# Q and k pieces taken from PSUM by TensorE and ScalarE, a third bank pair for the wide scores, and filler matmuls

## What is computed

```python
qkv = x @ w_attn                       # 16 query heads of 8, one k and one v head of 8
att = softmax(mask(q k^T * scale))     # causal, 256 x 256 per head
x = x + (att @ v) @ w_proj             # on layernorm(x)
sim = einsum(q', keys)                 # 8 heads, 2 x 32 key scores per token
sx, ix = top_k(sim[0], 16); sy, iy = top_k(sim[1], 16)
scores, pk = top_k(all pairs sx + sy, 16)
h = gelu(xn . table_down[indices]) * softmax(scores)
x = x + sum(h * table_up[indices])
```

## Time and profile before

| | us |
|---|---|
| median of 3 runs | 883.25 (880.9 to 883.42) |
| profiled execution | 882.14 |
| its span | 880.4 |
| TensorE busy | 725.1 (82%) |
| VectorE busy | 752.1 (85%) |
| ScalarE busy | 704.5 (80%) |
| GpSimd busy | 646.6 (73%) |
| mean granted TensorE clock | 0.953 of full speed |

### The profile page before, as it was taken

The page is one execution under the profiler, slowest core; times in us unless marked ns, Lnnn a source line. Parts: engine busy times, 40 slices in busy tenths (PEclk is TensorE's granted clock), DMA queues, the critical chain, the costliest instruction groups (busy, mean ns, idle before and its releaser), DMA issues.

```text
span 880.4 us, 20930 instructions
## 1 busy us (share of the span) xinstructions
PE 725.1 (82%) x6084; PEld 483.2 (55%) x6116; DVE 752.1 (85%) x2962; ACT 704.5 (80%) x959; POOL 646.6 (73%) x370
## 2 busy tenths in 40 slices
PE   3987688897979798897979798897979788876767
PEld 2653345564746465564646465564646465553646
DVE  4428799899989898999989898989989898988884
ACT  1365788989889898989989898989989898869471
POOL 3111596997969697997969697897969696887662
PEclk9897889999999999999999999999999999799988
DMA  6223021210302121210302121210302021000000
GB/s 180 45 39 73 1 59 21 53 31 18 66 0 65 18 58 25 52 31 12 71 0 65 18 58 25 52 31 11 72 0 65 18 53 26 25 8 6 15 6 7
DMA packets 34736, 32.53 MB, mean 37 GB/s; under 512 B 5520, under 2 KB 32784, under 8 KB 32976
## 3 DMA queue, kind: packets, MB, share of 16 engines
q1 hardware_dynamic: 34608, 32.12, 16.4%
q10 hardware_dynamic: 96, 0.02, 0.0%
HBM read 19.93 MB, written 5.24 MB: 29 GB/s over the span
## 4 chain that ended last, share of the span: by engine, by line
PE 29%; issue 29%; DVE 21%; ACT 10%; POOL 7%; ACTq 1%; another core or an unknown queue 1%; POOLq 1%; DVEq 1%; DMA 0%
DVE prob L1050 8%; PE score L1373 6%; ACT prob L744 4%; POOL acc L510 4%; DVE late_scores L905 3%; ACT late_scores L610 3%; PE misc L1444 3%; PE misc L1290 2%; PE score L1270 2%; PE score L1385 2%; DVE halves L899 2%; DVE ranked L949 1%; PE score L1327 1%; PE misc L1393 1%; PE score L1272 1%
## 5 line engine op out<-in xcount | busy, mean ns | idle before, releaser
L510 POOL TENSOR_TENSOR acc<-acc,prob 128x1024 f32<-128x1024 f32 x184 | 435.4, 2366 | 16.2 <-DVE prob L1050 0.5
L1050 DVE SCALAR_TENSOR_TENSOR prob<-score,cut,prob 128x1024 f32<-128x1024 f32 x256 | 317.9, 1279 | 31.9 <-ACT prob L744 30.6
L744 ACT ACTIVATE prob<-score,neg_lse,unit 128x1024 f32<-128x1024 f32 x256 | 301.4, 1203 | 27.6 <-PE score L1373 22.4
L1373 PE MATMUL score<-sel,pieces_t 128*128 128x512 f16 x512 | 161.6, 402 | 57.6 <-DVE prob L1050 54.9
L510 POOL TENSOR_TENSOR acc<-prob 128x1024 f32<-128x1024 f32 x32 | 75.6, 2362 | 100.7 <-DVE prob L1050 100.7
L637 ACT ACTIVATE probs<-score 128x512 f32<-128x512 f32 x192 | 109.8, 597 | 24.2 <-PE score L1272 20.2
L1373 PEld LDWEIGHTS score<-sel,pieces_t 128*128 128x128 f16 x512 | 40.5, 102 | 118.8 <-DVE prob L1050 107.6
L1327 PEld LDWEIGHTS score<-xn_kept,wdt 128*128 128x128 f32 x480 | 72.4, 191 | 29.7 <-issue 6.7
L1327 PE MATMUL score<-xn_kept,wdt 128*128 128x128 f32 x480 | 85.0, 278 | 3.9 <-DVE prob L1050 3.5
L1444 PEld LDWEIGHTS misc<-wu,gated_t 128*128 128x128 f32 x480 | 65.1, 199 | 13.8 <-DVE qk_rest L892 5.8
L1240 PE MATMUL score<-k_ahead,q_ahead 128*128 128x256 bf16 (+1 forms) x512 | 68.9, 246 | 2.9 <-ACT late_scores L610 0.7
(11 more groups left out here) (147 smaller groups left out, 1424.7 us busy)
## 6 DMA issues: line engine op xcount, KB each, us to landing
q_scratch<-qk_piece SPq DMA_DIRECT2D x16, 192.0 KB, 2.1
q_ahead<-q_scratch SPq DMA_DIRECT2D x16, 192.0 KB
q_stack<-q_scratch SPq DMA_DIRECT2D x16, 192.0 KB
xin<-x SPq DMA_DIRECT2D x16, 128.0 KB, 2.4
q_ahead<-q_scratch SPq DMA_DIRECT2D x16, 128.0 KB
q_stack<-q_scratch SPq DMA_DIRECT2D x16, 128.0 KB
xres<-x SPq DMA_DIRECT2D x16, 128.0 KB, 2.6
x_kept<-x SPq DMA_DIRECT2D x16, 128.0 KB, 2.0
```

What stands on the lines that cost most here:

```text
L510: eng.tensor_tensor(acc[:, j, :], so_far, prob[:, j * FH + h, :], ALU.add).then_inc(acc_added, FH - h if last else 1)
L744: eng.activation(prob[:, g, :], score[g % BUFS][:, :], ACT.Exp, bias=neg_lse[:, j, h:h + 1], scale=unit[:, :]).then_inc(prob_made, 1)
L1050: eng.scalar_tensor_tensor(prob[:, g, :], score[g % BUFS][:, :], cut[:, j, h:h + 1], prob[:, g, :], ALU.is_ge, ALU.mult).then_inc(prob_mas ...
L1373: ins = eng.matmul(score[g % BUFS][:, cols], pieces_t[:, j, h, :], sel[:, cols], start=True, stop=True)
```

## The change

1. **Pieces of q and k.** VectorE's and GpSimd's subtractions go. TensorE subtracts the piece just copied from the bank itself, with a negated identity (`take_piece`); ScalarE copies the middle and the low piece from the bank.
2. **Scale.** The scale of the exp is rounded to a power of two and put into the selection matrix (`sel_unit`, bfloat16); the exp keeps only its bias tile. The cut is scaled by VectorE (`scale_cut`).
3. **Bank pairs.** The six wide score groups use banks 2, 1, 2, 1, 2, 0. The first stands ahead of the value products, and tile 1's transposed sum ahead of the last group and of the piece transposes.
4. **Softmax steps** are done once for both tiles, with the copied maxima in `score[0]`.
5. **Filler matmuls** (`keep_busy`): 9, 4 and 3 where TensorE waits.
6. The order on ScalarE and VectorE follows these.

```diff
-                eng.activation(qk_piece[:, 1, :], qk_rest[:, :], ACT.Copy).then_inc(qk_middle, 1)
+                eng.activation(qk_piece[:, 1, :], misc[1][:, :], ACT.Copy).then_inc(qk_middle, 1)
+            def qk_low_piece(b):
+                eng.wait_ge(qk_last_made, every(qk_last_made, b))
+                eng.activation(qk_piece[:, 2, :], misc[1][:, :], ACT.Copy).then_inc(qk_low, 1)
...
-                eng.activation(prob[:, g, :], score[g % BUFS][:, :], ACT.Exp, bias=neg_lse[:, j, h:h + 1],
-                               scale=unit[:, :]).then_inc(prob_made, 1)
+                eng.activation(prob[:, g, :], score[g % BUFS][:, :], ACT.Exp,
+                               bias=neg_lse[:, j, h:h + 1]).then_inc(prob_made, 1)
...
+            def take_piece(b, n):
+                if n == 0:
+                    eng.wait_ge(setup_dve, 4)
+                    eng.wait_ge(qk_high, every(qk_high, b))
+                else:
+                    eng.wait_ge(qk_middle, every(qk_middle, b))
+                eng.matmul(misc[1][:, :], neg_ident_bf[:, :], qk_piece[:, n, :], start=False,
+                           stop=True, skip_group_check=True).then_inc(qk_last_made if n else qk_rest_made, 1)
```

ScalarE's order in an iteration:

```diff
+                if m:
+                    max_scores_back(i + 2, 0)
                 if a:
                     invert_sums(i + 1)
                 if m:
-                    copy_v(i + 2)
-                    max_scores_back(i + 2, 0)
                     max_scores_back(i + 2, 1)
-                if f:
-                    best_exp(i, 0)
-                if m:
                     max_scores_back(i + 2, 2)
                     max_scores_back(i + 2, 3)
                 if a:
                     x2_back(i + 1)
                 if f:
+                    best_exp(i)
+                if m:
+                    max_scores_back(i + 2, 4)
+                    max_scores_back(i + 2, 5)
+                if f:
+                    log_sum(i)
                     pieces_back(i, 0)
-                if m:
-                    max_scores_back(i + 2, 4)
-                if f:
-                    log_sum(i, 0)
-                if m:
-                    max_scores_back(i + 2, 5)
-                if f:
                     pieces_back(i, 1)
+                if f:
+                    pair_probs(i, 0, 0)
                 if a:
                     xn_back(i + 1)
-                if f:
-                    pair_probs(i, 0, 0)
-                    best_exp(i, 1)
                 if p:
                     xhat_back(i + 3)
                 if f:
                     pair_probs(i, 0, 1)
-                    log_sum(i, 1)
+                if m:
+                    copy_v(i + 2)
+                if f:
                     pair_probs(i, 0, 2)
...
                 if f:
                     pair_probs(i, 0, 7)
+                if p:
+                    qk_low_piece(i + 3)
                 if m:
                     max_back(i + 2)
```

VectorE's order:

```diff
                     select_pairs(i, 0)
-                    shift_best(i, 0)
                     sum_pairs(i, 1)
-                if d and f and not a:
+                    select_pairs(i, 1)
+                if a:
+                    make_y(i + 1)
+                if d and f:
                     gate(i - 1, 0)
                 if f:
-                    select_pairs(i, 1)
-                if a:
-                    make_y(i + 1)
-                if d and a:
-                    gate(i - 1, 0)
+                    shift_best(i)
                 if a:
                     norm_x2(i + 1)
                 if p:
                     ln1(i + 3)
-                if f and not a:
-                    shift_best(i, 1)
-                if f:
-                    sum_best(i, 0)
+                if f:
+                    bound_sizes(i)
+                    sum_best(i)
                 if d and f:
                     gate(i - 1, 1)
-                if f and a:
-                    shift_best(i, 1)
-                if f:
-                    log_sum_exp(i, 0)
-                if m:
-                    fold_max(i + 2, 0, 3)
-                if f:
-                    bound_sizes(i)
-                if m:
-                    fold_max(i + 2, 3, 4)
-                if f:
-                    sum_best(i, 1)
-                if m:
-                    fold_max(i + 2, 4, 5)
+                if m:
+                    fold_max(i + 2, 0, 1)
+                if f:
+                    log_sum_exp(i)
+                if m:
+                    fold_max(i + 2, 1, 2)
                 if f:
                     place_cut(i)
                 if m:
-                    fold_max(i + 2, 5, 6)
+                    fold_max(i + 2, 2, 4)
+                if f:
+                    scale_cut(i)
+                if m:
+                    fold_max(i + 2, 4, 6)
                 if f:
                     mask(i, 0, 0)
-                    log_sum_exp(i, 1)
                     mask(i, 0, 1)
                     mask(i, 0, 2)
                     mask(i, 0, 3)
                     mask(i, 0, 4)
                     mask(i, 0, 5)
-                if p:
-                    qk_remainder(i + 3)
```

TensorE's order:

```diff
+                if m:
+                    scores_for_max(i + 2, 0)
                 if a:
                     weigh_values(i + 1, 0, max_t_made, i + 1)
                     weigh_values(i + 1, 1, max_t_made, i + 1)
                 if m:
-                    scores_for_max(i + 2, 0, d)
-                    scores_for_max(i + 2, 1)
+                    scores_for_max(i + 2, 1, d)
+                    scores_for_max(i + 2, 2)
                 if d and f:
                     acc_transposes(i - 1, 0)
...
                     project_y(i + 1, y_t_made, i + 1)
+                if m:
+                    scores_for_max(i + 2, 4)
+                if d and f and a:
+                    acc_transposes(i - 1, 1, m)
+                if m:
+                    scores_for_max(i + 2, 5)
                 if f:
                     if a:
                         piece_transposes(i, 0, y_t_made, every(y_t_made, i + 1))
                     else:
                         piece_transposes(i, 0, sim_kept, every(sim_kept, i))
+                    if m:
+                        eng.wait_ge(x2_made, every(x2_made, i + 1))
+                        keep_busy(misc[1], 9)
                     piece_transposes(i, 1, piece_t_made, at(piece_t_made, i, 1))
-                if d and f and a:
-                    acc_transposes(i - 1, 1, m)
-                elif f and d:
+                if f and d and not a:
                     sum_late_tile()
...
                     for n in range(4, 7):
+                        if p and n == 6:
+                            take_piece(i + 3, 0)
                         pair_scores(i, 0, n, a, m)
...
                 if p:
+                    take_piece(i + 3, 1)
                     keep_busy(misc[0], 2)
...
                     if p:
-                        reader, of_batch = qk_rest_made, i + 3
+                        reader, of_batch = qk_low, i + 3
```

More of the change, by code:

```diff
@@ L7 @@
 FP16 = mybir.dt.float16
+INT32 = mybir.dt.int32
 ALU = mybir.AluOpType
@@ L42 @@
 WIDE_STEPS = 6
+MAX_BANK = (2, 1, 2, 1, 2, 0)
 BUFS = 3
@@ L203, in build @@
         qk_rest_made = signal("qk_rest_made")
+        qk_last_made = signal("qk_last_made")
         qk_middle = signal("qk_middle")
@@ L764, in prologue @@
                 xhat_back(2)
+                max_scores_back(1, 0)
                 invert_sums(0)
-                for w in range(2):
-                    max_scores_back(1, w)
+                max_scores_back(1, 1)
                 x2_back(0)
@@ L1197, in fold_keys @@
                 eng.wait_ge(weights_in, 6 * 16)
+                eng.wait_ge(max_kept, every(max_kept, 0))
                 for l in range(LISTS):
@@ L1228, in scores_for_max @@
                     eng.wait_ge(ahead_in, every(ahead_in, b))
+                    if later(b):
+                        eng.wait_ge(att_probs, at(att_probs, b, 0))
+                elif w == 1:
                     if d:
                         eng.wait_ge(act_made, every(act_made, b - 3))
-                elif w == 1:
-                    if later(b):
-                        eng.wait_ge(att_probs, at(att_probs, b, 0))
-                else:
+                elif w < 5:
                     eng.wait_ge(max_kept, at(max_kept, b, w - 1))
+                elif later(b - 1 if isinstance(b, int) else b):
+                    eng.wait_ge(shifted_made, every(shifted_made, b - 2))
                 for u in (2 * w, 2 * w + 1):
-                    bank = score[1 + w % 2][:, (u % 2) * BANK:(u % 2 + 1) * BANK]
+                    bank = score[MAX_BANK[w]][:, (u % 2) * BANK:(u % 2 + 1) * BANK]
                     nh, nk, h0, j = (4, P, 4 * u, 0) if u < 4 else (2, T, 2 * (u - 4), 1)
@@ L1357, in pair_scores @@
                     eng.wait_ge(piece_t_made, at(piece_t_made, b, j + 1))
+                    if not later(b):
```

(5 more changed lines are left out.)

163 lines of the change are left out of this document (84 added, 79 removed).

## The result

The changed kernel takes **901.88 us** (median, 899.79 to 902.68) against 883.34 for the kernel before on the same chip: ratio 1.0208, 95% interval 1.0183 to 1.0234. It is slower, as forecast, by 18.5 us where the forecast had about 11. The median lies inside the range (871 to 902) by 0.1, at its edge, and above the likeliest case's own range (887 to 899). The profiled execution spans 899.8 us, 19.4 more than before.

The account below looks back on a forecast made before the run. The prediction took a loop of waits across engines as the bound, GpSimd's and ScalarE's loops nearly equal. 11 x 0.95 = 10.5, -2.5 and +4.2 gave +12.2 on 882.14: 894 us, range 871 to 902, likeliest case 887 to 899.

Parts of the forecast that it names:

- The first score group ahead: On TensorE, value products now await all twelve exps: +0.2 us on the path to xhat, bounds 0 and +0.54.
- GpSimd beside the folds: GpSimd's rstd, centring and scaling take 3.63 us instead of 2.97 beside VectorE's earlier fold: +0.66, bounds 0 and +1.3.
- The exps: On ScalarE, one operand tile fewer makes each exp 0.09 us cheaper: 1.02 start to start instead of 1.11.
- The low piece on ScalarE: ScalarE's new copy of q and k's low piece ends at 510.31; the expert output starts at 510.36 instead of 508.73.
- TensorE's queue: Expert output and scores of heads 9 to 12 queue behind the low piece; last mask ends at 522.53, +0.95 per period.
- rival C: Fillers don't hold the clock at line 1317's key products: 0.9 us in half the periods, 899; chance 0.13 with D.
- The prologue: The stretch before the batches' regular periods: no change, 0, with bounds -1 and +2 us.
- i = 13 and 14: These iterations carry no pieces of q and k and keep VectorE's gain of 1.25 us each: -2.5.
- The last iteration: Transposes for batch 14's second tile wait behind ScalarE's merged exp and log: +4.9, less 0.7 for fewer steps, +4.2 us.
- Rival A: GpSimd's loop is the bound, saving 1.16 us per period: 871; chance 0.29 together with B's fast form.
- B: Later fold misses rstd and TensorE keeps ahead: no change (0.13), 887 form (0.05), or fast 876 (0.29 with A).
- D: The operand pointer costs nothing, or the exp isn't shortened: +0.5 us per period, 900; chance 0.13 together with C.

Follow-up runs that it names:

- e7: Changed kernel with the first score group put back behind the value products on TensorE, as in the kernel before; 896.89 us.
- e10: Changed kernel with the expert output one place later, six fillers instead of two in two pauses, and GpSimd's rstd ahead of two scalings of xn; 894.14 us.
- e11: Kernel e1 with GpSimd's rstd of xhat issued ahead of the two scalings of xn, nothing else; 889.93 us.
- e8: Changed kernel with a scale tile of ones given back to each of the 256 exps; 911.17 us.
- e1: Changed kernel with the q and k part alone undone (VectorE's remainder and GpSimd's low piece back); 882.42 us.
- e3: Changed kernel with the expert output's four groups one place later on TensorE, the scores of head 9 ahead of the first; 885.66 us.
- e5: Changed kernel without the new 9, 4 and 3 filler products behind the piece transposes and heads 0 and 1; 910.34 us.
- e4: Changed kernel with six filler products instead of two in each of TensorE's two pauses beside heads 6 and 7; 895.72 us.
- e12: Changed kernel with ScalarE's low piece behind head 9's exp, the expert output two places later, and six fillers in the first pause; 903.83 us.
- e2: Kernel before with the q and k part alone put in; banks, order and exps as they were; 922.22 us.

## Why the prediction was right, and where it was not

- **The first fold** was put 18.48 behind the period's start (493.95 less 475.47); it came at 18.46. Right.
- **The first score group ahead** (+0.2): e7 gives 0.13. Right.
- **GpSimd beside the folds** (3.63 for three operations): 3.88, since the centring was stretched too (1.22). With the 0.25 that this is short, xhat comes 1.14 later instead of 0.86. Right in kind. e10 and e11 show that a delay of xhat comes through to the period. The Trainium skill (GPSIMD Engine Reference, Specifications) names contention with VectorE instructions of two SBUF inputs; these traces agree.
- **The exps** (1.11): 1.12. Right, and e8 prices them at 0.70 per period. In e1 xhat is ready at 22.55 instead of 21.4, and the nine masks still start within 0.13 of where they did before: the cheaper exps and the key products at the high clock together gave back what the fold took. e1 doesn't tell the two apart. (The terms up to the exp of head 4 add up to 5.78, not 5.76; it changes nothing.)
- **The low piece on ScalarE** was put at an end of 34.84 and the expert output at 34.89; they came at 35.01 and 35.06. **TensorE's queue** behind it: the last mask's end was put at 47.06 and came at 47.19. The period was forecast at +0.95, measured +1.07, and e3 takes it away whole. This is the step on which the direction rested, and it was right.
- **The clock** is the step that failed. The forecast's sum had no term for it; rival C had 5 us for it, at the key products on line 1317, with a small chance. There the fillers worked (592 to 697 ns each; e5). It fell instead on the expert output, in three of eleven periods, for 5.0 us (e4). C's place was wrong, and it came together with the forecast's mechanism rather than in its stead. That its 5 us agrees is luck: C had 0.9 us in half of the periods, and 1.65 in three of eleven was measured.
- **The prologue** (0, bounds -1 and +2) took +3.5, outside the bounds. TensorE's 30 fillers now end at 21.35, it waits 4.45 for the transfer of q, and its first scores run at the low clock; the first attention scores start at 45.3 instead of 42.1. But kernels with this same prologue put the first copy anywhere from 72.95 (e3) to 77.89 (e12), and their first attention scores from 43.4 to 48.3, so a single figure isn't to be had.
- **i = 13 and 14**: -3.4 for -2.5. **The last iteration**: the sum of the late tile starts 17.2 behind the last copy instead of 11.8, +5.4 (predicted +4.9), but only 2.5 of it reaches the end, where 4.2 was forecast.

The terms that were off, in the sum: clock +5.0, prologue and first iterations +3.6, periods +1.3, the ends -2.6. Together they are 7.3, which takes the forecast's +12.2 to the measured 19.4 but for rounding. That the median still fell inside the range, by 0.1, is luck: its upper end came from leaving out the ends of C and D, and left no room for a prologue of +3.5. Rival A (faster) failed where it was said to decide: the low piece's copy would have had to end before 508.7 in the old time scale; it ended at 510.5. B (the fold misses rstd) fell with rstd's 1.58, and D (the exp isn't shortened) with the 1120 ns.

## What to carry to other kernels

When a step moves to another engine, ask who waits for its last signal and what stands behind that waiter in its queue: here 0.64 us of copying held eight products and the scores of four heads, and moving the waiter behind one score group was worth 16 us, 5 of them by way of the clock. A trial of a remedy is read by its own target (when is xhat ready?) before the total: e10 moved the collision and did not remove it. And a run can hold two losses that come and go together: a kernel that takes away only one of them (e4) told them apart.

## What was not expected of the hardware

- GpSimd operations of quite different size are stretched alike beside VectorE's bf16 folds: two elements per partition from 0.70 to 1.58 beside one fold of 1.22, a 128x128 scaling from 0.80 to 2.95 beside two of them. The delay follows the folds, not the operation. Beside the gate, with one input in PSUM, the same scalings keep their 0.80 (changed kernel, 504.25).
- A pattern as steady as 50.66 within 0.02 can hold the low clock in every third period at the same place, with the same busy times as the periods without it, and a shift of the work by a microsecond (e3) or twice 0.44 us of fillers (e4) removes it from all.
- The same q and k part costs 39 us in the kernel before (e2) and some 19 in the changed one (against e1), and moving the expert output by one place takes 18 and 16 of it.
